# Attention over keys in 16 groups: the turns of the sums moved from their copies, every maximum item put in front of the weighed sum, and two reciprocal buffers

## The reference, cut to what matters

```python
q = (x @ Wq.T)  # B, 32 heads, T = 1024, 16
k = (x @ Wk.T)  # B, 8 groups of keys, T, 16
v = (x @ Wv.T)
scores = jnp.einsum('bhgtd,bhkd->bhgtk', qg, k) / math.sqrt(DH)
scores = jnp.where(causal[None, None, None], scores, jnp.finfo(jnp.float32).min)
attn = jax.nn.softmax(scores, axis=-1)
ctx = jnp.einsum('bhgtk,bhkd->bhgtd', attn, v)
```

## Time and profile before

| | us |
|---|---|
| median of 3 runs | 1766.54 |
| lowest, highest | 1763.19, 1767.64 |
| the profiled execution | 1761.45 |
| its span (first to last instruction) | 1759.7 |
| attention stage, first scores of group 0 to those of group 15 | 1175.4 to 1655.3 |
| busy in the span: TensorE, VectorE, ScalarE, GpSimd | 1444.5, 1140.1, 600.2, 339.6 |

### The profile page before, as it was taken

How to read it: one execution, slowest core, us unless ns; L and a number is a source line. 1 busy time by engine, 2 the same in 40 slices (tenths; PEclk the granted TensorE clock), 3 DMA queues, 4 the chain that set the end, 5 groups by cost and what they waited for, 6 DMA issues and landing times. The chain is left out here.

```text
span 1759.7 us, 21845 instructions
## 1 busy us (share of the span) xinstructions
PE 1444.5 (82%) x7034; PEld 940.3 (53%) x7034; DVE 1140.1 (65%) x2432; ACT 600.2 (34%) x859; POOL 339.6 (19%) x382
## 2 busy tenths in 40 slices
PE   0399889899847783899999999488888889988869
PEld 0366657567535562677777776344344344343337
DVE  5577875768745545455555544388888887888427
ACT  4224223242213330111111111016656665666632
POOL 2243433333412220000000000002122221221211
PEclk9999979889767896899999999659999998999989
DMA  7200000100013533000001000221221311311032
GB/s 260 103 1 1 24 25 1 48 1 24 1 65 130 165 106 122 31 19 24 19 19 31 11 14 0 48 42 29 46 39 29 56 29 29 56 29 29 1 133 83
DMA packets 49624, 84.54 MB, mean 48 GB/s; under 512 B 9411, under 2 KB 17681, under 8 KB 49530
## 3 DMA queue, kind: packets, MB, share of 16 engines
q1 hardware_dynamic: 42898, 78.39, 16.5%
q10 hardware_dynamic: 6632, 4.97, 0.9%
HBM read 58.54 MB, written 24.26 MB: 47 GB/s over the span
## 5 line engine op out<-in xcount | busy, mean ns | idle before, releaser
L1517 ACT ACTIVATE f_prob<-f_bank 128x1024 f32<-128x1024 f32 (+3 forms) x384 | 298.7, 810 | 190.8 <-PE f_bank L1617 190.8
L1598 PE MATMUL f_bank<-f_kst,f_qst 64*128 64x512 f32 (+3 forms) x768 | 268.7, 430 | 49.5 <-DMA f_qst<-f_kst 18.6
L1538 DVE CUSTOM_DVE_ANT_0 f_bank<-f_bank,f_mask 128x128 f32<-128x128 f32 (+3 forms) x512 | 239.8, 517 | 67.7 <-PE f_bank L1598 54.4
L1598 PEld LDWEIGHTS f_bank<-f_kst,f_qst 64*128 64x128 f32 x768 | 136.9, 198 | 225.4 <-DVE f_mx_first L1541 91.9
L1617 PE MATMUL f_bank<-f_qst,f_kst 64*128 64x512 f32 (+3 forms) x768 | 205.2, 405 | 2.7 <-ACT f_prob L1517 2.5
L1485 POOL TENSOR_SCALAR_AFFINE_SELECT f_prob<-f_prob 128x256 f32<-128x256 f32 x256 | 103.2, 406 | 441.1 <-ACT f_prob L1517 438.5
L1541 DVE TENSOR_REDUCE f_mx_first<-f_bank 128x1 f32<-128x512 f32 x256 | 168.4, 685 | 16.2 <-PE f_bank L1598 13.0
L1635 PE MATMUL f_bank<-f_prob,f_vst 128*32 128x512 f32 (+3 forms) x1536 | 173.1, 524 | 1.7 <-ACT f_prob L1517 1.3
L37 PE MATMUL d_bank<-xtl,d_wgh 128*128 (+1 forms) x352 | 143.3, 407 | 8.8 <-DMA d_zz<-z_gu_scr 8.8
L1187 ACT ACTIVATE d_hs<-d_bank 128x512 f32<-128x512 f32 (+1 forms) x44 | 26.3, 598 | 348.4 <-PE d_bank L39 348.4
L39 PE MATMUL d_bank<-xth,d_wgh 128*128 (+1 forms) x352 | 140.8, 400 | 0.0
(11 more groups left out here) (226 smaller groups left out, 2757.7 us busy)
## 6 DMA issues: line engine op xcount, KB each, us to landing
f_qst<-q_scr SPq DMA_DIRECT2D x32, 384.0 KB, 6.9
q_scr<-c_qh SPq DMA_DIRECT2D x32, 256.0 KB
wst<-L_ffn_w SPq DMA_DIRECT2D x6, 1024.0 KB, 5.8
f_kst<-k_scr SPq DMA_DIRECT2D x32, 192.0 KB, 5.5
d_qw<-L_ffn_qweight_gu SPq DMA_DIRECT2D x40, 128.0 KB, 2.6
xall<-L_attn_x SPq DMA_DIRECT2D x2, 2048.0 KB, 16.3
xb<-L_attn_x SPq DMA_DIRECT2D x4, 1024.0 KB, 5.3
x_d<-xb SPq DMA_DIRECT2D x4, 1024.0 KB, 4.3
```

Of the source, the lines that this page charges most:

```text
L1517: act.activation(prob[:, c // 2 % 2, c % 2 * 2:c % 2 * 2 + 2, lo:], score_bank[c % 2][:, :, lo:], ACT.Exp, scale=D ** -0.5).then_inc(exp_d ...
L1538: dve.tensor_tensor_reduce(sc, sc, mask[:, CH - w:CH], 1.0, LEAST, ALU.add, ALU.max, mx[:, u, h % 2, h // 2, q:q + 1]).then_inc(spare_free, 1)
L1598: pe.matmul(spare[v][:, 0:w], qst[r, u, h // 2, q * P:q * P + P], kst[r, u, at:at + w], start=True, stop=True).then_inc(spare_ps, 1)
```

## The change

The turn of the group before moves from step 2 to step 5, the turn of the first half from step 10 to step 13; ScalarE's copies stay in steps 2 and 10, under names of their own. On TensorE all tasks of a step come before the weighed sum. The reciprocals have one buffer for each half, and the drain ahead of the reciprocal goes. The step in which GpSimd copies the values of the next group (3) keeps its place under a new name.

```diff
--- before.py
+++ after.py
@@ -1290,7 +1290,9 @@
 
 UNITS = [(0, k) for k in range(QPH)] + [(1, k) for k in (0, 4, 5, 6, 7, 1, 2, 3)]
 NU, NC = len(UNITS), 2 * len(UNITS)
-HEAD = 3
+COPY_LAST, TURN_LAST = 2, 5
+COPY_FIRST, TURN_FIRST = 10, 13
+VALUES = 3
 
 ITEMS = [(2 * i + par, q, at, min(CH, (q + 1) * P - at)) for i in range(HG // 2) for q in range(QB)
          for at in range(0, (q + 1) * P, CH) for par in range(2)]
@@ -1306,7 +1308,6 @@
     return slice(par * HALF_ROWS, (par + 1) * HALF_ROWS)
 
 TURN_MAXIMA = 19
-TURN_FIRST_HALF = 10
 LOADED = 6 * 16
 LEAST = -3.0e38
 SPARE = 3
@@ -1331,9 +1332,9 @@
     for c in range(NC):
         if c < TURN_MAXIMA and ahead >= 1:
             out += [(c, "items", s) for s in beside(c)]
-        if c == HEAD - 1:
+        if c == TURN_LAST:
             out.append((c, "turn the group before", None))
-        if c == TURN_FIRST_HALF:
+        if c == TURN_FIRST:
             out.append((c, "turn half", None))
         if c >= TURN_MAXIMA and ahead >= 2:
             out += [(c, "early", s) for s in beside(c)]
@@ -1364,7 +1365,7 @@
         mx_first = sb("mx_first", [P, 2, 2, QB])
         mt = sb("mt", [HG * QB, STACKS, P], F32R)
         ctxt = sb("ctxt", [P, HALF, CH])
-        rden = sb("rden", [P, QPH, HG])
+        rden = sb("rden", [P, HALF, QPH, HG])
         bank = ctx.enter_context(nc.psum_tensor("f_bank", [P, 8, 512], F32))
         spare = [bank[:, 0], bank[:, 1], bank[:, 7]]
         score_bank = [bank[:, 2:4], bank[:, 4:6]]
@@ -1420,12 +1421,12 @@
                         at += 1 if first else 0
                         bank_at = use(k, at) if isinstance(n, int) else use(0, at) + k * len(FULL)
                         todo.append((use(n, at), bank_at % SPARE, task, s))
-                step(c, group(j, k), todo, None if first else group(j, k - 1), group(j, k + 1), group(j, k + 2))
+                step(c, group(j, k), todo, group(j, k - 1) if k > 0 else None, group(j, k + 1), group(j, k + 2))
 
             assert len(FULL) % SPARE == 0
             for n in range(NG):
                 for c in range(NC):
-                    run(c, 0, n, n == 0 and c < HEAD)
+                    run(c, 0, n, n == 0 and c <= TURN_LAST)
             tail(group(0, NG - 1), use(NG - 1, len(tasks(0))))
 
         block = ctx.enter_context(nc.Block())
@@ -1484,7 +1485,7 @@
                     p = prob[:, c // 2 % 2, c % 2 * 2:c % 2 * 2 + 2, span(h, k):span(h, k) + P]
                     pool.affine_select(out=p, in_=p, compare_op=ALU.is_ge, fill=0.0, base=0,
                                        pattern=[[0, 2], [1, P]], channel_multiplier=-1).then_inc(masked, 1)
-                if c == HEAD and ahead_of(n) > 0:
+                if c == VALUES and ahead_of(n) > 0:
                     pool.wait_ge(av_done, n * NU + 2)
                     values(after)
             values(group(0, 0))
@@ -1507,9 +1508,9 @@
             def step(c, g, todo, before, after, second):
                 n = g[0]
                 lo = span(*UNITS[c // 2])
-                if any(task == "turn the group before" for _, _, task, _ in todo):
+                if c == COPY_LAST and before is not None:
                     turn(before[0], 1)
-                if c == 2 * QPH + 2:
+                if c == COPY_FIRST:
                     turn(n, 0)
                 if c % 2 == 0:
                     act.wait_ge(av_done, n * NU + c // 2 + 1)
@@ -1554,13 +1555,12 @@
             def normalize(g, h, number, v):
 
                 n = g[0]
-                dve.drain()
                 dve.wait_ge(spare_ps, number + 1)
                 turned = spare[v].rearrange("p (b h d) -> p b h d", h=HG, d=2 * D)
-                dve.reciprocal(rden[:, :, :], turned[:, :, :, D])
+                dve.reciprocal(rden[:, h], turned[:, :, :, D])
                 dve.drain()
                 dve.tensor_tensor(ctx_sb[:, bass.ds(n, 1), h * QPH:(h + 1) * QPH].rearrange("p n b (h d) -> p (n b) h d", d=D),
-                                  turned[:, :, :, 0:D], rden[:, :, :].rearrange("p b (h o) -> p b h o", o=1).broadcast_to([P, QPH, HG, D]),
+                                  turned[:, :, :, 0:D], rden[:, h].rearrange("p b (h o) -> p b h o", o=1).broadcast_to([P, QPH, HG, D]),
                                   ALU.mult).then_inc(spare_free, 1)
 
             def step(c, g, todo, before, after, second):
@@ -1659,12 +1659,11 @@
                             turn(g, 0, number, v)
                         else:
                             turn(before, 1, number, v)
-                run(todo[:1])
+                run(todo)
                 if c > 1 and c % 2 == 1:
                     weighed(g, c // 2 - 1)
                 elif c == 1 and before is not None:
                     weighed(before, NU - 1)
-                run(todo[1:])
 
             def tail(g, number):
                 weighed(g, NU - 1)
```

## The result

The changed kernel takes 1864.17 us (median of 4 runs, 1861.77 to 1871.37), the kernel before 1767.09 in the same comparison. The ratio is 1.0557, 95% interval 1.0535 to 1.0578: 97 us slower. The forecast was 1783, the range ended at 1799. The profiled execution of the changed kernel is the longest of its four (1871.37) and that of the kernel before one of its shortest, so their spans stand 110 us apart and not 97. The direction was right and the size wrong: 16 us were forecast.

The account below looks back on a forecast made before the run. Bound: a loop of TensorE and VectorE over three banks, VectorE's time with waits setting group length. 14 groups at +1.2 us (16.8) plus 0.3, low clock unchanged, give 1778.5 profiled; 5.1 more for the median: 1783, range 1767 to 1799.

Parts of the forecast that it names:

- Part 3: All items in front of the weighed sum: VectorE's waits come to 6.4 us a group, group 32.1 against 30.9.
- term (a): Bank hand-over: TensorE starts 0.06 us after VectorE ends the piece of work three uses back.
- The signs that the prediction named for its waits: VectorE waits about 0.7 us before item 27 (step 8), and 0.6 or more before items 3 and 7.
- Low clock stays at its 13.5: Attention groups: low-clock loss stays 13.5 us, between 0 and 2.8 in each of 14 groups.
- More: Rival: longer TensorE idle between weighed sums of steps 17 and 19 lowers every group's clock; 1808 or 1795 us; chance 0.10.
- (c): Time a weighed sum holds TensorE: 0.99 us for 512 columns, 0.78 for 384, then 0.57 and 0.36.
- (d): Delay of an item by the score pair ahead: 0.33 us for 512 columns, 0.28 for 384, then 0.23 and 0.17.
- Part 2: Turns moved to steps 5 and 13: the delay makes nobody wait; items no longer late behind their old places.
- (b): From an item to the weighed sum behind it on TensorE: 0.33 us, 0.25 more with a turn between.
- Part 1: Two reciprocal buffers, no first drain: reciprocal starts 0.17 us earlier per turn, 0.34 a group.
- Faster: Rival: item order is free as scores run beside the item before; group 29.1 us, median 1741; chance 0.12.
- No change: Rival: waits behind the turns in steps 5 and 13, 0.37 + 0.76 us, don't appear; 1768 us; chance 0.08.

Follow-up runs that it names:

- f5: Changed kernel with the score matmuls of odd steps issued twice, those of step 19 four times: 1795.91 us, ratio 1.0166 to the kernel before.
- f2: Kernel before with the score matmuls of step 19 alone issued three times, 4 matmuls more in a group: 1750.25 us, ratio 0.9930.
- f1: Changed kernel with the score matmuls of every odd step issued twice, 24 matmuls more in each group: 1796.19 us, ratio 1.0199 to the kernel before.

## Why the prediction was wrong in size

**Part 3, direction and place: right.** The weighed sum that filled TensorE's wait for a bank has been pushed behind the wait, and the scores of the next step behind it. The order alone is 78 us slower, and VectorE's waits stand before the items named.

**Part 3, size at 2.4 GHz: short.** 32.9 and not 32.1. Most of it is in term (a), the 0.06 from a freed bank to the next matmul. It was read from a plain reduction (item 9); behind a masked one the short accumulator read frees the bank, and the matmul starts 0.11 to 0.12 after the end of the reduction. The rows on record had this too: item 14 ends at 1403.51 + 0.43 = 1403.94 and the turn that waits for its bank starts at 1404.06, and from the end of an item at 1395.41 to the maxima it is 0.11. VectorE and TensorE in step 7 of group 7, changed kernel (item 23 on VectorE first; then TensorE):

```profile
1463.76 0.73 DVE L1539 CUSTOM_DVE_ANT_0 f_bank<-f_bank,f_mask 128x512 f32<-128x512 f32 x1
1464.41 0.14 DVE L1539 DVE_READ_ACCUMULATOR2_ANT f_mx<- 128x1 f32 x1
```

```profile
1462.86 0.27 PE L1598 MATMUL f_bank<-f_kst,f_qst 64*128 64x128 f32 x1
1463.96 0.32 PE L1598 MATMUL f_bank<-f_kst,f_qst 64*128 64x128 f32 x1 [0.83 <-DVE f_mx L1539]
1464.61 0.38 PE L1598 MATMUL f_bank<-f_kst,f_qst 64*128 64x256 f32 x1 [0.32 <-DVE f_mx L1539]
1464.92 0.64 PE L1635 MATMUL f_bank<-f_prob,f_vst 128*32 128x256 f32 x8
1465.49 0.50 PE L1617 MATMUL f_bank<-f_qst,f_kst 64*128 64x512 f32 x2
1465.82 0.33 PE L1598 MATMUL f_bank<-f_kst,f_qst 64*128 64x384 f32 x2
```

The reduction ends at 1464.49, the accumulator read at 1464.55, and the item that waits for this bank starts at 1464.61. The rest is as worked out: two waits for banks (0.83, 0.32), the weighed sum 0.31 behind the last item, 0.57 long, the scores 0.33. Eleven hand-overs at 0.05 to 0.07 more are 0.6 to 0.7 a group. Redone by the prediction's measure from VectorE's starts in the full-clock group of f5, the waits come to about 7.2 where it had 6.4. Single steps are off by -0.02 to +0.14, and step 17 has no wait at all, so the rest of the 0.8 is spread over the other terms. The signs that the prediction named for its waits hold there: VectorE's idle time is 0.62 before item 27, 0.67 before item 3 and 0.72 before item 7.

**Low clock stays at its 13.5: the step that failed.** The 13 groups 1 to 13 took 415.2 us before and take 512.4 after, in the profiled executions: +97 of the 110 us between these two. Of the 97, 13 x 2.0 = 26 are the order at 2.4 GHz, and 71 are low clock, 13.5 us before and 85 after (512.4 less 13 x 32.9). So a term that the sum kept at its old size grew by 71 us, while all that the sum worked out moved by 26. The rival "More" named the mechanism and had 0.10; its bound was wrong too, for it took the worst group of before, 2.8 us, as the worst there can be. In the new order a group loses 85 / 13 = 6.5. The reason it gave against itself, that groups 7 and 9 run the same instructions at 1.00 and at 0.90, says the opposite of what I took from it: where the same group runs at either clock, little is needed to move it, as the four matmuls of f2 do in the other direction. The bound should have been the price of a hand-over at 1.2 GHz: 1.86 and 0.60 for the weighed sum and the scores and not 1.00 and 0.33, 1.1 more on each of the wide ones. Over the twelve weighed sums and score pairs of the prediction's list, with its widths, that is about 10.8 us for a group wholly at 1.2 GHz (an estimate: 0.86 of the 9.4 in its terms (c) and 0.82 of the 3.3 in (d)), well above the 6.5 measured at a mean clock of 0.75. That the loss feeds on itself (longer waits of VectorE, later banks, longer idle of TensorE) fits with low stretches of 10 us and more, where the kernel before has none above 7 in these groups; no run separates this from the first cause.

The Trainium skill, TensorE: Matmul & The Clock Gate, section A second HAM failure mode: psum-queue depth-cycling, had told of such a loss in a kernel that goes round its PSUM buffers with short idle times. The traces here agree, with waits of 0.52, 0.83 and 0.32 us on TensorE ahead of the fall at 1466.4, and f1 and f2, which put matmuls ahead of such waits, bring the clock from 0.75 to 0.94 and from 0.96 to 1.00.

**Part 2, moved turns: right in sign, small.** 0.2 a group at 2.4 GHz alone. But "in front of a weighed sum they add 0.25 to (b)" was priced at full clock only, some 0.5 a group or 7 us: under the new order it is 15 to 18 us of the whole.

**Part 1, the drain: right in its 0.17, wrong in that it always counts.** Alone it brings nothing, as VectorE waits for TensorE right after; with moved turns 0.3 a group, where 0.34 was forecast. With no drain the reciprocal starts 0.60 after the reduction, 0.08 before its recorded end. The sentence of the Trainium skill, VectorE: DVE Perf Modes, section The DRAIN you can't avoid, that was weighed there doesn't hold for this pair; the same section adds that an operation which is not held starts earlier, and the trace agrees with that.

**The rivals.** Faster, with scores that cost their items nothing: fallen, 1465.49 to 1465.82 is 0.33 again. No change, with hidden turns: fallen, VectorE waits 0.41 and 0.72 behind the two turns in the full-clock group of f5.

**The range.** Laid end to end, its terms (4 to 25, clock -8 to +10) around 1766.5 give 1763 to 1802 and not 1767 to 1799. That changes nothing here: 85 us of low clock lie far outside either.

## What to carry to other kernels

In a loop of two engines over few buffers, the long piece of work belongs into the wait for a buffer, not behind it; put it in front of the last producer of a round, and count what stands between it and the next one. Before costing a change of order, look at the granted clock of each repeat of the same loop: where equal repeats run at different clocks, as here at 1.00 and 0.90, a small change can move the clock of all of them, and the change has to be priced at both levels. A few repeated matmuls where TensorE waits anyway are a cheap test of this, and in this kernel, in the right step, they are also a gain.

## What was not expected of the hardware

More work made TensorE faster: 24 matmuls more in a group took 68 us off the kernel, four more in step 19 took 13 us off the kernel before (1763.03 to 1750.25). Two turns a group, 0.59 us of TensorE each in front of or behind a weighed sum, moved 15 to 18 us (1864.17 against 1846.45), more than the 7 us that 0.25 each comes to. The clock of the groups differs too, 0.75 with the turn in front against 0.78 with it behind, but how much of the time goes through the clock is not shown. And an edit that shortens every full-clock group by 0.5 us can show as no difference at all, with the mean clock gone from 0.96 to 0.94.
